# Cross-attention scores from f16 halves in two passes, with a new order of the turn on PE, ACT and DVE

## The reference

```python
x = x + attn(layernorm(x), w_qkv, w_o, ...)   # 16 query heads, 4 key heads of 128, causal, rope
x = x + xattn(layernorm(x), ctx, Wq, Wk, Wv)  # below
x = x + ffn(layernorm(x), W_up, W_gate, W_down)  # ternary weights, silu

# xattn: 32 heads of 16, every query row sees all 361 context rows
q = rmsnorm(x @ Wq.T per head); k = rmsnorm(ctx @ Wk.T per head); v = ctx @ Wv.T per head
attn = softmax(q @ k.T * 16 ** -0.5); out = attn @ v
```

## Time and profile before

| | us |
|---|---|
| median of 3 runs | 1376.08 (1375.34 to 1378.37) |
| the profiled execution | 1380.27 |
| its span | 1378.3 |
| PE busy | 1314.2 (95%) |
| DVE busy | 774.7 (56%) |
| ACT busy | 643.9 (47%) |
| POOL busy | 299.3 (22%) |

### The profile page before, as it was taken

The page is one execution under the profiler, slowest core; times in us unless marked ns, Lnnn a source line. Parts: engine busy times, 40 slices in busy tenths (PEclk is TensorE's granted clock), DMA queues, the critical chain, the costliest instruction groups (busy, mean ns, idle before and its releaser), DMA issues.

```text
span 1378.3 us, 27489 instructions
## 1 busy us (share of the span) xinstructions
PE 1314.2 (95%) x10976; PEld 872.7 (63%) x10976; DVE 774.7 (56%) x1881; ACT 643.9 (47%) x1458; POOL 299.3 (22%) x281
## 2 busy tenths in 40 slices
PE   8879999999999999999999999999999799999996
PEld 7656666666666666566666666666666455565543
DVE  5987775777667784534344444444335894444422
ACT  4633354333333354366666666666666323232321
POOL 0654452444344441211101112111101121000000
PEclk9999999999999999999999999999999999999999
DMA  8400000000000002012211111111113520000000
GB/s 271 161 1 1 1 1 0 1 0 2 0 1 1 1 2 113 25 67 67 69 46 46 47 46 46 46 46 46 51 53 113 176 92 23 1 23 1 23 1 29
DMA packets 23604, 60.00 MB, mean 44 GB/s; under 512 B 1214, under 2 KB 10811, under 8 KB 20405
## 3 DMA queue, kind: packets, MB, share of 16 engines
q1 hardware_dynamic: 23477, 58.24, 12.6%
HBM read 54.96 MB, written 3.28 MB: 42 GB/s over the span
## 4 chain that ended last, share of the span: by engine, by line
PE 84%; DVE 7%; issue 5%; ACT 2%; POOL 1%; DVEq 0%; POOLq 0%; ACTq 0%
PE A L1704 18%; PE A L1610 12%; PE A L1667 10%; PE C L2048 10%; PE C L1735 6%; PE B L1752 5%; PE C L1653 3%; PE C L1638 3%; PE A L1685 2%; PE A L2067 2%; PE B L2067 2%; PE A L1619 2%; PE B L1630 2%; PE B L1721 2%; PE B L1646 2%
## 5 line engine op out<-in xcount | busy, mean ns | idle before, releaser
L1704 PE MATMUL A<-wxhl,arena 128*122 128x512 f16 x1152 | 265.5, 380 | 0.0
L1704 PEld LDWEIGHTS A<-wxhl,arena 128*122 128x122 f16 x1152 | 149.7, 134 | 88.7 <-issue 8.3
L2048 PE MATMUL C<-arena 128*128 128x375 f16 (+1 forms) x1024 | 186.5, 335 | 2.1 <-DVE arena L1207 2.1
L1610 PE MATMUL A<-arena,wxhl 128*125 128x512 f16 (+1 forms) x780 | 176.7, 384 | 6.5 <-DVE arena L1288 4.3
L518 POOL TENSOR_TENSOR arena<-arena,region 122x512 f32<-122x512 f32 (+2 forms) x61 | 62.9, 1062 | 420.1 <-DVE region L1163 420.1
L2048 PEld LDWEIGHTS C<-arena 128*128 128x128 bf16 x1024 | 100.0, 98 | 78.0 <-issue 4.0
L1610 PEld LDWEIGHTS A<-arena,wxhl 128*125 128x125 f16 (+1 forms) x780 | 105.7, 138 | 67.3 <-DVE arena L1288 4.8
L747 ACT ACTIVATE arena<-C 122x1600 f32<-122x1600 f32 x96 | 144.4, 1504 | 8.2 <-PE C L1735 6.7
L493 POOL TENSOR_TENSOR region<-tub 125x512 f32<-125x512 f32 (+1 forms) x65 | 82.5, 1269 | 250.7 <-DVE tub L1028 249.2
L663 ACT ACTIVATE region<-C,negm 100x100 f32<-100x100 f32 x256 | 84.3, 354 | 102.2 <-DVE negm L1074 102.2
L1667 PE MATMUL A<-arena,stageb 128*125 128x512 f16 (+1 forms) x416 | 123.8, 379 | 0.7 <-ACT arena L731 0.7
(11 more groups left out here) (178 smaller groups left out, 2191.8 us busy)
## 6 DMA issues: line engine op xcount, KB each, us to landing
stageb<-in_wffn SPq DMA_DIRECT2D x16, 768.0 KB, 4.8
arena<-in_ctxt SPq DMA_DIRECT2D x16, 722.0 KB, 4.6
stageb<-in_wffn SPq DMA_DIRECT2D x6, 1024.0 KB, 4.8
wxhl<-in_wffn SPq DMA_DIRECT2D x6, 1024.0 KB, 4.8
arena<-in_wqkv SPq DMA_DIRECT2D x4, 1024.0 KB, 15.1
arena<-in_wx SPq DMA_DIRECT2D x3, 1024.0 KB, 8.4
out_x<-xres SPq DMA_DIRECT2D x12, 250.0 KB
xres<-in_x SPq DMA_DIRECT2D x1, 2250.0 KB
```

The costliest lines, as they stand in the source:

```text
L1610: ins = pe.matmul(A[j % 2][0:m, :], xp[:, k, at:at + m], wp[:, j, k, :], start=(n == 0), stop=(n == 11))
L1704: ins = pe.matmul(A[(par + n) % 2][0:KC, :], xp[:, k, c * KC:(c + 1) * KC], wp[:, 1 if n < 4 else 2, k, :], start=(i == 0), stop=(i == 11))
L2048: ins = pe.matmul(C[2 * (e % 2) + half][:, 0:cols], wf[:, 3 * (e // 4) + half, k, (e % 4) * 128:(e % 4 + 1) * 128], part[:, k, 0:cols], st ...
```

## The change

The normed keys and queries are split into f16 halves before they are turned, and turned as f16. Keys carry both halves of a head in 32 rows (16 hi, 16 lo); queries are laid down twice, the hi half of the query against both and the lo half against both, in two accumulating passes. The parity mask and its doubled columns go. Key copies move from ACT to DVE, and the orders of all three queues are new. Its core:

```diff
-WARM, FILL = 14, 14
+WARM, FILL = 6, 14
-        e = carve([KC, 6, HT * S])
+        e = carve([KC, 12, 4 * S])
@@ ACT
-            def keys_back(b, t):
-                act.activation(kT[:, t], B[0][:, 0:CTXP], ACT.Copy).then_inc(sig["a_T"], 1)
+            def query_hi(i, par):
+                act.wait_ge(*count("g_qn", i, 1))
+                q = raw[par][0:n, 3]....unsqueeze(2).broadcast_to([n, XH, 2, XD])
+                act.activation(qx[0:n, 0]..., q, ACT.Copy)   # 1024 columns
+            def key_hi(b, c, par):
+                act.wait_ge(*count("g_kn", b, c + 1))
+                act.activation(kx[c][:, :, 0, :], raw[par][0:KC, c]..., ACT.Copy)   # 512 columns
@@ ACT turn, from exp2(b, 3) on
                 exp2(b, 4)
                 if end < 2:
+                    if q_tile(b + 1) is not None:
+                        query_hi(q_tile(b + 1), odd)
+                    values(b + 1, 0, odd)
+                    key_hi(b + 1, 0, odd)
+                    key_hi(b + 1, 1, odd)
+                exp2(b, 5)
+                if end < 2:
+                    key_hi(b + 1, 2, odd)
+                    magnitudes(b, 0, par)
                     values(b + 1, 1, odd)
+                    magnitudes(b, 1, par)
+                    values(b + 1, 2, odd)
                 if end < 1:
-                    magnitudes(b, 1, par)
+                    ctx_hi(b + 2)
...
-                exp2(b, 5)
-                if end < 2:
-                    values(b + 1, 2, odd)
-                    keys_back(b + 1, 0)
                 out_back(b, 2)
-                if end < 1:
-                    ctx_hi(b + 2)
+                out_back(b, 3)
+                if x2_tile(b) is not None:
+                    keep_q(x2_tile(b), par)
                 if end < 2:
                     exp2(b + 1, 0)
-                out_back(b, 3)
-                if end < 2:
-                    keys_back(b + 1, 1)
@@ DVE
+            def query_lo(i, par):      # 1024 columns: lo = q - hi, waits for a_qh
+            def key_lo(b, c, par):     # 512 columns: lo = k - hi, waits for a_kh
+            def keys_back(b, t):
+                dve.wait_ge(*count("pe_T", b, t + 1))
+                dve.tensor_copy(kT[:, 2 * t:2 * t + 2]..., B0h[:, 0:2 * CTXP])
-            def queries_back(i):
+            def queries_back(i, f):    # twice a tile: copies out of B0h, no mask
@@ DVE turn: keys_back(b, 2) first, keys_back(b, 3) ahead of square_sums(b + 1, 3)
@@ or, at the end, of scales3; then after x2_lo
+                if end < 2 and q_tile(b + 1) is not None:
+                    query_lo(q_tile(b + 1), odd)
                 if o2_tile(b) is not None:
                     add_cross(o2_tile(b), 0)
+                if end < 2:
+                    key_lo(b + 1, 0, odd)
+                    if q_tile(b + 1) is not None:
+                        queries_back(q_tile(b + 1), 0)
+                    key_lo(b + 1, 1, odd)
+                    key_lo(b + 1, 2, odd)
                 if end == 1:
                     row_scales3(0)
...
+                    queries_back(q_tile(b + 1), 1)
+                if end < 2:
+                    keys_back(b + 1, 0)
...
                 if end < 1:
                     ctx_lo(b + 2)
+                if end < 2:
+                    keys_back(b + 1, 1)
@@ DVE prologue
+                elif j == 1:
+                    columns()
                 proj(0, j)
                 if j == 1:
-                    columns()
-                elif j == 2:
-                    dve.wait_ge(ld_r, 16)
-                    tables(slice(1, 4), ((0, 2),))
-                elif j == 3:
-                    tables(slice(1, 4), ((1, 0),))
+                    dve.wait_ge(ld_r, 16)
+                    tables(slice(1, 4), ((0, 2), (1, 0)))
@@ PE
+            def turn_queries(i, f):    # 8 f16 transposes for each of the two halves
+            def turn_heads(b, t):      # 6 f16 transposes
             def scores2(b, u):
...
-                for f in range(2):
-                    t, c = divmod(2 * u + f, NC)
-                    for r in range(RT):
-                        ins = pe.matmul(C[r][0:KC, f * 2 * S:(f + 1) * 2 * S], kT[32 * r:32 * r + 32, t, ...],
-                                        qms[b % 2][32 * r:32 * r + 32, t]..., start=True, stop=True)
+                for f in range(4):
+                    g, c = divmod(4 * u + f, NC)
+                    for half in range(2):
+                        for r in range(RT):
+                            ins = pe.matmul(C[r][0:KC, f * S:(f + 1) * S], kT[32 * r:32 * r + 32, g, ...],
+                                            qTs[b % 2][32 * r:32 * r + 32, g, half, :],
+                                            start=(half == 0), stop=(half == 1))
@@ PE turn
-                scores2(b, 1)
                 if end < 2:
                     project2(b + 1, 1, odd)
+                scores2(b, 1)
...
                 scores2(b, 5)
                 if end < 2:
+                    project2(b + 1, 6, odd)
+                if o2_tile(b) is not None:
+                    pe.wait_ge(*count("d_on", o2_tile(b), 1))
+                if end < 2 and q_tile(b + 1) is not None:
+                    turn_queries(q_tile(b + 1), 0)
+                attend2(b, 2, par)
+                if end < 2 and q_tile(b + 1) is not None:
+                    pe.wait_ge(*count("d_qT", q_tile(b + 1), 1))
+                    turn_queries(q_tile(b + 1), 1)
+                attend2(b, 3, par)
+                if end < 2:
+                    if q_tile(b + 1) is not None:
+                        pe.wait_ge(*count("d_qT", q_tile(b + 1), 2))
+                    turn_heads(b + 1, 0)
                 if x2_tile(b) is not None:
                     pe.wait_ge(*count("a_v2", b + 1, 2))
                     project_q(x2_tile(b), par)
                 if end < 2:
-                    pe.wait_ge(*count("a_T", b + 1, 2))
+                    scores2(b + 1, 0)
+                    turn_heads(b + 1, 1)
+                    pe.wait_ge(*count("d_T", b + 1, 2))
                 if o2_tile(b) is not None:
                     out_turn(o2_tile(b), 1)
```

More of the change, by code:

```diff
@@ L284, in build @@
         osum = carve([TW, DM])
+        kx = [carve([KC, XH, 2, XD], F16) for _ in range(2)]
         carve = carver(region2)
@@ L848, in _ @@
                 values(0, c, 0)
+            query_hi(0, 0)
+            for c in range(NC):
+                key_hi(0, c, 0)
             ctx_hi(1)
-            keys_back(0, 0)
-            keys_back(0, 1)
             x2_hi(1, B[0])
@@ L860, in turn @@
                 odd = 1 - par
-                exp2(b, 1)
                 if end < 2:
                     keep_raw(b + 1, 1, odd)
-                keys_back(b, 2)
+                exp2(b, 1)
                 if end < 2:
@@ L1432, in _ @@
             normed2(1, rs1[:, 0:1])
+            query_lo(0, 0)
+            for c in range(NC):
+                key_lo(0, c, 0)
+            queries_back(0, 0)
+            queries_back(0, 1)
             ctx_lo(1)
-            queries_back(0)
+            keys_back(0, 0)
+            keys_back(0, 1)
             add_attn(TL - 1, A[0])
@@ L1440, in turn @@
                 odd = 1 - par
+                if end == 2:
+                    dve.wait_ge(*count("a_abs", NB - 1, 3))
+                    dve.tensor_reduce(fsc[:, 0:3], asum[:, :, :, 0], AX.X, ALU.add).then_inc(d_fsc, 1)
+                keys_back(b, 2)
                 if end < 2:
                     square_sums(b + 1, 1)
-                else:
-                    dve.wait_ge(*count("a_abs", NB - 1, 3))
-                    dve.tensor_reduce(fsc[:, 0:3], asum[:, :, :, 0], AX.X, ALU.add).then_inc(d_fsc, 1)
                 if x2_tile(b) is not None:
@@ L1453, in turn @@
                     x3_lo(0, 0, A[0])
+                keys_back(b, 3)
                 if end < 2:
@@ L1725, in scores2 @@
                 if u == 0:
-                    pe.wait_ge(*count("a_T", b, 1))
-                    pe.wait_ge(*count("d_qT", last_tile(b), 1))
+                    pe.wait_ge(*count("d_T", b, 1))
                 if u > 0:
@@ L1942, in between @@
             def between(g):
-                if g == 2:
+                if g == 1:
                     pe.wait_ge(*count("a_pT", b, 4))
                     turn_queries(0, 0)
+                elif g == 2:
+                    pe.wait_ge(*count("d_qT", 0, 1))
+                    turn_queries(0, 1)
             project_out(TL - 1, b, A[0], between)
[L1950 to L1954, removed]
+            pe.wait_ge(*count("d_qT", 0, 2))
+            turn_heads(0, 0)
+            pe.wait_ge(*count("d_T", 0, 1))
+            turn_heads(0, 1)
+            pe.wait_ge(*count("d_T", 0, 2))
             x2_turn(1, B[0])
@@ L1974, in turn @@
                     pe.wait_ge(*count("d_x2", 1, 1))
-                turn_heads(b, 2, par)
+                turn_heads(b, 2)
                 if end < 2:
@@ L1980, in turn @@
                 attend2(b, 0, par)
```

(6 more changed lines are left out.)

105 lines of the change are left out of this document (51 added, 54 removed).

## The result

The changed kernel takes 1399.71 us (median of 4 runs, 1395.44 to 1400.62) against 1376.51 us for the kernel before in the same comparison (4 runs): the ratio is 1.0165, 95% interval 1.0147 to 1.0182. It is slower by 23.2 us. The forecast was 1388.7 with a range of 1366 to 1408: the sign and the two waits that carry it came out, the size was half.

A forecast was written before the change was run, and what follows sets the result against it. PE, busy 95% of the span, was taken as the bound. Terms -29.8 + 6.4 + 4.8 + 10.7 + 22.5 + 3.3 - 5.3 = +12.6 us gave 1392.9 profiled, 1388.7 as median; range 1366 to 1408.

The forecast's parts named there:

- Score unit: Cross-attention scores on PE: a unit falls from 0.89 to 0.57 us, saving 0.31; 96 units give -29.8 us.
- Rival 2: Score units' weight loads are not hidden: unit 0.87, total 1417 us; half hidden 0.75, 1406; chance 0.12.
- Transposes: PE's f16 transposes: keys unchanged at 0.32 us, query tiles +6.4 in all; separate placings add +4.8.
- rival 3: Key and query transposes on PE: f16 ones cost what f32 ones do, 19 us more, 1408; chance 0.08.
- The forecast's terms for a full turn without a hole: Per turn on PE: score units' saving, +0.49 for a query tile's transposes, +0.34 for separate placing of scores and transposes.
- Wait after the last key transposes: PE waits for DVE's key copy with no projection between: 0.84 us a turn, together +10.7 (+5 to +16).
- Wait before attend group 3: PE waits for ACT's out_back, queued behind small operations: 1.2 to 2.1 us a turn, +22.5 in all.
- Rival 1: Before attend group 3, ACT reaches out_back in time, the 22.5 us vanish: 1366 us, faster; chance 0.22.
- the prologue: Table products placed before GpSimd's operation avoid a 4.4 us DVE product; projection 4 starts earlier: -5.3 us.
- rival 4: The prologue gains nothing if the table's operands arrive later than 33 us: 1394 us; chance 0.1.
- Fewer warm-up matmuls: In the prologue, 6 in the source instead of 14: between -1.5 and +2 us, taken as 0.
- what turn 15 was to cost: Part of the last turns' +3.3 us: 1.6 saved in score units not banked, and DVE's keys_back delaying the scales 1.2.

The follow-up runs named there:

- the narrow load: Changed kernel with score weights of 96 key columns instead of 122, leaving some scores uncomputed: 1393.68 us in one run.
- both moves: Changed kernel with second key transposes ahead of the first scores and out_back(b, 2) ahead of the last values copy and context's half: 1373.02 us, ratio 0.9969.
- taking the cover back: Changed kernel with the next batch's second key transposes issued ahead of its first scores on PE: 1393.75 us, ratio 1.0123.
- The experiment: Changed kernel with out_back(b, 2) on ACT issued ahead of the last values copy and the context's half: 1379.68 us, ratio 1.0025.
- The run with the products one step later: Against the kernel with both moves, the prologue's rope products and second tile's statistics moved one step later: 1365.77 us, ratio 0.9918.

## Why the prediction was right, and what it missed

Against the profiled execution of before the forecast was +12.6; +18.85 came.

- **Score unit**: 0.57 forecast, 0.58 measured, and the narrow load bears out its reason. Rival 2 is out; the chip did not keep the longer gap between load-and-matmul pairs that the Trainium skill gives ("TensorE: Matmul & The Clock Gate", "Back-to-back issue gap") with four groups of rows at work, at 56 ns a round of four.
- **Transposes**: keys 0.33 for six (0.32 forecast), rival 3 is out. Two groups of eight query transposes take 0.54 and 0.61 with no wait in the version with both moves, 1.15 against 0.97 forecast with the change of division: +0.18 in 13 tiles, 2 us too low. The forecast's terms for a full turn without a hole were -1.86 + 0.49 + 0.34 = -1.03; that version measures -0.97.
- **Wait after the last key transposes**: from the transposes' start to the output transposes 750.78 - 749.65 = 1.13, against 0.59 + 0.57 + 0.05 = 1.21 in the forecast. The key copy took 538 ns against 570 (the row below; busy us, mean ns). In all 13.1 us of waits, and taking the cover back returned 6.0.

```profile
L1198 DVE COPY arena<-B 128x732 f16<-128x732 f16 x64 | 34.4, 538 | 101.3 <-PE B L1773 101.3
```

- **Wait before attend group 3**: 24.3 measured, 22.5 forecast; 1.20 in a full turn (1.2 forecast), 1.63 without the tile's transposes (1.5), 2.05 without a query tile (2.1). Rival 1 was wrong: ACT, idle for half the span, is full just there. The experiment makes it 20.0 of the 23.2.
- **The step that failed is the prologue**: -5.3 was given, with rival 4 for the case that the operands come later than 33 us. They came at 34.09, and the gain between the traces was 1.0 at turn 0 and 0.2 at the values projection. I had seen the clash that the move removes and not asked in which order DVE meets the transfer. The run with the products one step later won 7 us: the gain was there, one place further down the queue. Fewer warm-up matmuls, taken as 0, were not tried alone.
- **Not in the sum at all**: the granted clock. Two of the three longest holes were followed by a stretch at 0.50 (3.2 us together), which no term had. Over whole executions it is more: the mean granted clock has a median of 0.990 in the 23 executions of the kernel before that stand beside the first four runs, 0.984 in the changed kernel, and 0.981 to 0.985 in every version with the change. An estimate from these: 0.006 of 1400 us is 8 us of full clock, at most that much of the 23.2, and with both moves (0.983) 9 us, which could be what the 3 us of gain lack. No run changes the clock alone, so this share stays open.

The 6.25 us between forecast and profile divide so. Up to unit 2 of turn 0 the changed kernel is 1.0 earlier (595.28 against 596.28) instead of 5.3: +4.3. From there to unit 2 of turn 15 (1080.35 against 1062.86) it loses 18.5, of which 3.2 is the clock's; the terms for these turns sum to 12.6 + 5.3 - 1.2 = 16.7, with 1.2 for what turn 15 was to cost (3.3 less turn 14's 0.5 and 1.6 of unbanked units, which the 29.8 had counted): 15.3 measured without the clock, -1.4. The rest of turn 15 costs 18.8 - 17.5 = 1.3, and that this meets the forecast is in part luck: it holds the 3.16 us for which attend group 2 waits for `add_cross`. The new order on PE puts this wait two attend groups earlier, the old one had it behind attend group 3, where PE did not wait for it; in turn 15 no queries are turned that would need it. The forecast had only the key copy ahead of the scales there. Between the medians the difference is 23.2 and not 18.85. The profiled execution of before lay 3.8 above its median, and that of after 0.6 below. The clock fits this: 0.987 in that execution against the median of 0.990 is, as an estimate, 4 us of full clock. The stretches at 0.50 fall in different places in each execution and move single profiles by several us.

## What to carry to other kernels

When a change gives back matmul time on an engine without holes, write down for each of its waits which instructions stand between the producer's trigger and the wait; two groups moved in the queues turned 23 us of loss into 3 of gain here, with the arithmetic untouched. A copy that frees a PSUM bank for the bound engine goes ahead of work that nobody waits for in this turn. When a wait on a transfer is moved forward in an in-order queue, list what stood in front of it before: that work now waits for the transfer too.

## What the runs showed of the hardware

- 32-row matmuls on four groups of rows: a round of four takes 56 ns with 122-column f16 weights and 100 streamed columns. With 96-column weights the unit falls from 0.58 to 0.50 us, and putting two matmuls of one group of rows one behind the other costs 0.01.
- A hole of 2.05 us on TensorE was followed by some 3.4 us at granted clock 0.50 in two of three equal places (874, 1038, not 712). In the profile of the version with both halves on one group of rows, holes of 2.06 us in the same three places were followed by none.
- A DVE copy of 732 f16 columns out of PSUM took 538 ns, less than 375 f32 columns.
- Behind the prologue, two operations on 4 columns each took DVE 6.61 us together beside GpSimd's weight half (L530), and 0.28 when that was over. In the kernel before the same pairs took 1.75 and 2.19, so where such a clash falls moves with a few us of schedule. The runs here did not try to part them:

```profile
63.10 6.61 DVE L1085 TENSOR_SCALAR negm<-smax 100x4 f32<-100x4 f32 x2
...
71.55 0.28 DVE L1085 TENSOR_SCALAR negm<-smax 100x4 f32<-100x4 f32 x2
```

```profile
65.62 4.06 POOL L530 TENSOR_TENSOR arena<-stageb,arena 128x2048 f16<-128x2048 f32 x1
```
